# Turning f32 rows on the tensor engine: a product with a scaled identity, or a scaling on ACT and a transposition

## The chip, the cores and the metric

The kernel runs on one core of one Trainium2 chip. The metric is the device time of one execution in microseconds (us); the kernel before takes 4029.41 us (median of 3 runs, 4027.86 to 4030.45). The engines named below are PE (TensorE, products into PSUM; PEld are its weight loads), DVE (VectorE), ACT (ScalarE), POOL (GpSimd) and SP (SyncE, which here only issues DMAs). Each works through its own instructions in order; semaphores order them across engines.

## The reference, cut to what matters

```python
# x: (8, 16, 512, 512) f32
# layer 0
x = x + irfftn(complex_conv3x3(rfftn(_gn(x)), w_real, w_imag, b_real, b_imag))
# layer 1
x = x + mean_filter(_gn(x), 15)      # 15x15 box, zero padded, per channel
# _gn(v): per image and group of 2 channels, (v - mean) / sqrt(var + 1e-5)
```

Only layer 1 is concerned: the image is normalised, averaged over 15x15 pixels, and added to itself.

## The kernel before, in words

The eight images are done one after the other. An image stays in SBUF as `img`, 128 partitions (8 bands of rows x 16 channels) by T = 64 row steps by 512 columns: row step u holds row u of every band. So a sum over rows of the image is a sum over u, with a hand-over to the neighbouring band at the borders, and a sum over columns runs along the free axis.

Layer 0 rewrites `img` in place. Layer 1 then forms the box in two parts, row step by row step:

- The sum over 15 rows is never held. PSUM accumulates the whole box in `p0[0]`, and each step u adds only the difference between the row that enters and the row that leaves.
- For u from 8 to 56 (49 steps, `R < u < T - R` with R = 7) both rows are in the same band: POOL's `difference` (L1353) writes `diff[u % 2]` = row u+7 less row u-8. For the 7 steps at either border the two rows lie in different bands, and PE combines them by two products with permutation matrices ("dual-term" steps); step 0 is a sum made earlier (`head`, `tail`).
- PE turns the difference, 4 blocks of 128x128 f32: `turn_row` (L655) takes the row's block as the stationary operand and a matrix as the moving one, into `turned_ps[u % 2]`. The matrix is an identity times the scale of the normalisation (`turn_mat["ident"]`, made once per image from column 10 of `sc`), so that turn and scaling are one. The two factors of an f32 product appear in the trace as two records per product.
- ACT copies the turned row to f16 (`high_part`, L844, recorded under L727), DVE writes the rest (`low_part`, L1213), together `parts[u % 2]`.
- PE's `box_row` (L677) multiplies both parts with a 0/1 band matrix, 8 products, and accumulates in `p0[0]`; DVE's `add_box` (L1226) adds the result to the image row, and SP stores it, two rows at a time.

PE's order is: turn u+1, box u, and, while another image follows, one half of the weighted row sums of the next image (`sum_part`, L491) from u = 17 on. Box u waits for the low part of u and for addition u-1, which reads the only accumulator. Turn u+1 waits for the low part of u-1. DVE's order is: low part u, addition u-1, and from u = 16 on the statistics of one row of the next image (`count_row`, L973). ACT issues the next image's loads, 4 rows in two DMAs after every fourth high part (`load_next`, L860). POOL's difference u waits for turn u-2, since it reuses the buffer.

All code is written out in this order; no scheduler moves anything. The last image has no successor: no sums, statistics or loads.

Of the kernel before, what the change touches and what calls it, by code (L numbers as in the profile page):

```python
# [36 lines left out]
P = 128  # L37
# [4 lines left out]
T = H // HB  # L42
# [5 lines left out]
R = K // 2  # L48
# [4 lines left out]
NDIFF = T - K  # L53
LAG = 16
NQ = W // P
# [97 lines left out]
def build(nc, x, w_real, w_imag, b_real, b_imag, tab, bd_dram, out):  # L153
    x_v = x.rearrange("b c (s hl t) w -> b s c hl (t w)", s=2, hl=HL)
    out_v = out.rearrange("b c (s hl t) w -> b s c hl (t w)", s=2, hl=HL)
    with ExitStack() as ctx:
        def sb(name, shape, dt=F32):
            return ctx.enter_context(nc.sbuf_tensor(name, shape, dt))

        def sem(name):  # L160
            return ctx.enter_context(nc.semaphore(name))
# [3 lines left out]
        tb = {n: sb(n, list(tab[n].shape), tab[n].dtype) for n in TABLES if n not in IN_DRAM}  # L165
# [13 lines left out]
        diff = [piece[s] for s in range(2)]  # L179
# [15 lines left out]
        turn_mat = {n: flat_bd[:, i * P:(i + 1) * P]  # L195
                    for i, n in enumerate(("ident", "neg_ident", "neg_prev", "next_"))}
# [18 lines left out]
        sc = sb("sc", [P, 28])  # L215
# [10 lines left out]
        turned_ps = [h_ps[:, s, :].rearrange("p (k m) -> p k m", k=NQ) for s in range(2)]  # L226
# [35 lines left out]
        moved, presummed, head_ready, tail_ready = sem("moved"), sem("presummed"), sem("head_ready"), sem("tail_ready")  # L262
# [1 line left out]
        mats_ready, mean_made, mean_spread = sem("mats_ready"), sem("mean_made"), sem("mean_spread")  # L264
        mean_kept, bordered = sem("mean_kept"), sem("bordered")
        turned, high_done, low_done, banded = sem("turned"), sem("high_done"), sem("low_done"), sem("banded")
        row_kept = sem("row_kept")
        row_out, stores_held, half_seen = sem("row_out"), sem("stores_held"), sem("half_seen")
        stored = [sem(f"stored{s}") for s in range(NS)]

# [134 lines left out]
        def _(pe):  # L405
# [75 lines left out]
            def sum_part(b, q, part):  # L481

                k, r = q * 2 // CHUNK, q * 2 % CHUNK
                if part == 0:
                    wait_rows(pe, b, 2 * q)
                    if r == 0:
                        pe.wait_ge(uvw_ready, b * NCH + k + 1)
                cols = slice(part * HALF, (part + 1) * HALF)
                for i in range(2):
                    w = uvw[k % 2][:, 4 * (r + i):4 * (r + i) + 4, :].rearrange("p j c -> p (j c)")  # L490
                    m = mm(uv_ps[i * HP:(i + 1) * HP, cols], w, img[:, 2 * q + i, cols],  # L491
                           start=(q == 0 and part == 0), stop=(q == T // 2 - 1 and part == 1),
                           skip_group_check=True)
                if r == CHUNK - 2 and part == 1:
                    m.then_inc(uv_summed, 1)

            def sum_rows(b, k):

                for q in range(k * CHUNK // 2, (k + 1) * CHUNK // 2):
                    for part in range(2):  # L500
                        sum_part(b, q, part)
# [151 lines left out]
            def layer1(b, follow):  # L653

                def turn_row(u, *terms):  # L655
                    for k in range(NQ):
                        for i, (mat, row) in enumerate(terms):
                            m = mm(turned_ps[u % 2][:, k, :], row[:, k * P:(k + 1) * P], mat,  # L658
                                   start=(i == 0), stop=(i == len(terms) - 1))
                    m.then_inc(turned, 1)  # L660

                def turn_step(u):

                    if u >= 2:
                        pe.wait_ge(low_done, b * T + u - 1)
                    if u <= R:
                        turn_row(u, (turn_mat["ident"], img[:, u + R, :]),
                                 (turn_mat["neg_prev"], img[:, u + T - R - 1, :]))
                    elif u < T - R:
                        pe.wait_ge(moved, b * NDIFF + u - R)  # L670
                        turn_row(u, (turn_mat["ident"], diff[u % 2]))
                    else:
                        pe.wait_ge(row_kept, b * R + u - (T - R) + 1)
                        turn_row(u, (turn_mat["next_"], kept_row[u - (T - R)]),
                                 (turn_mat["neg_ident"], img[:, u - R - 1, :]))

                def box_row(u):  # L677

                    pe.wait_ge(low_done, b * T + u + 1)
                    pe.wait_ge(row_out, PRIMED + b * T + u)  # L680
                    for k in range(NQ):
                        lo, hi = max(k * P - R, 0), min(k * P + P + R, W)
                        for l in range(2):
                            m = mm(p0[0][:, lo:hi], parts[u % 2][:, l, k, :],  # L684
                                   tb["band16"][:, lo - k * P + R:hi - k * P + R],
                                   start=(u == 0 and k == 0 and l == 0),
                                   stop=(u == T - 1 and k == NQ - 1 and l == 1), skip_group_check=True)
                    m.then_inc(banded, 1)


                pe.wait_ge(head_ready, b + 1)
                pe.wait_ge(tail_ready, b + 1)
                turn_row(0, (tb["ident"][:], head[:]), (tb["prev"][:], tail[:]))
                pe.wait_ge(mean_made, b + 1)
                mm(c_ps[:, 24:24 + C], sc[:, 24:25].broadcast_to([P, P]), mean_in[:], start=True, stop=True).then_inc(mean_spread, 1)
                pe.wait_ge(mats_ready, b * 4 + 2)
                for u in range(T):
                    if u + 1 < T:
                        if u + 1 == T - R:
                            pe.wait_ge(mats_ready, b * 4 + 4)  # L700
                        turn_step(u + 1)
                    box_row(u)
                    if follow and u > LAG:
                        sum_part(b + 1, (u - LAG - 1) // 2, (u - LAG - 1) % 2)
                if follow:
                    sum_part(b + 1, (T - LAG) // 2 - 1, 1)
                    for k in range((T - LAG) // CHUNK, NCH):
                        sum_rows(b + 1, k)
                    input_statistics(b + 1)
# [7 lines left out]
            with pe.Fori(0, B - 1) as b:  # L717
                layer0(b)
                layer1(b, True)
            layer0(B - 1)  # L720
            layer1(B - 1, False)


        @block.scalar
        def _(act):
            def copy(out_, in_):
                return nc.scalar.activation(out_, in_, ACT.Identity)  # L727
# [15 lines left out]
            def image(b, follow):  # L743
# [95 lines left out]
                def scaled(out_, in_, scale, bias=None):  # L839
                    if bias is None:  # L840
                        return nc.scalar.activation(out_, in_, ACT.Identity, scale=scale)
                    return nc.scalar.activation(out_, in_, ACT.Identity, bias=bias, scale=scale)

                def high_part(u):  # L844
                    if R < u < T - R or u == 0:
                        act.wait_ge(turned, b * T + u + 1)
                    else:
                        act.wait_ge(bordered, b * (2 * R) + (u if u <= R else u - (T - R) + R + 1))
                    if u >= 2:
                        act.wait_ge(banded, b * T + u - 1)  # L850
                    copy(parts[u % 2][:, 0], turned_ps[u % 2]).then_inc(high_done, 1)
# [8 lines left out]
                def load_next(t, rows, signal):  # L860

                    act.wait_ge(row_out, PRIMED + b * T + t + rows)
                    if t + rows <= NDIFF:
                        act.wait_ge(moved, b * NDIFF + t + rows)
                    for i in range(2):
                        act.dma_start(img[i * HP:(i + 1) * HP, t:t + rows, :].rearrange("p t w -> p (t w)"),
                                      x_v[b + 1, i, :, :, t * W:(t + rows) * W]).then_inc(signal, 16)

                for u in range(1, T):
                    high_part(u)  # L870
                    if u <= R:
                        copy(kept_row[u - 1], img[:, u - 1, :]).then_inc(row_kept, 1)
                    if follow:
                        k = u // CHUNK - 2
                        if u % CHUNK == CHUNK - 1 and 0 <= k < NCH - LAG // CHUNK:
                            load_next(k * CHUNK, CHUNK, loaded[k])
                        if u >= T - R and u % 2 == 1:
                            load_next(u - R - 2, 2, loaded_pair[(u - (T - R)) // 2])
                            if u >= T - R + 2:
                                load_next(u - 3, 2, loaded_pair[(u - (T - R)) // 2 + 3])  # L880
# [519 lines left out]
```

## Time and profile before

| | |
|---|---|
| median of 3 runs | 4029.41 us |
| the profiled execution's own time | 4030.95 us |
| its span (first to last instruction) | 4028.9 us |
| PE, DVE busy | 87%, 86% of the span |
| POOL, ACT busy | 65%, 59% |
| loads of 512 KB in the page's list of DMA issues (ACT's queue, L866) | 7.3 us from issue to landing, median |
| layer 1 of image 0: first turn to last low part | 512.71 to about 662 us |

The page's shares are of the whole span; layer 0 and layer 1 use the engines differently, so the stretches of layer 1 are read apart. A PE "matmul" row gives the time of an instruction including its latency, and matmuls overlap, so the time PE needs for a group is read from the starts of successive groups or from the chain. The granted clock is a share of 2.4 GHz. ACTq and SPq rows are DMA issues on the queue of ACT and SP.

### The profile page before, as it was taken

Reading aid. Unit: us, or ns where it says so; the run is one execution under the profiler, and the core shown is the slowest. Engines: PE = TensorE matmul, PEld = TensorE weight load, DVE = VectorE, ACT = ScalarE, POOL = GpSimd, SP = SyncE. Lnnn points to the kernel's source line nnn. Section 1 sums busy time; section 2 is a strip of 40 time slices with the busy share of each in tenths; the row PEclk is TensorE's granted clock in tenths of the full one; section 3 lists DMA queues with packets and bytes.
Section 4 is the critical chain, followed back from the end, with each engine's and each line's share of the span. In section 5 each row is a group of like instructions: output and inputs, shape, how many; then the busy total and the mean of one; then the engine's idle time right before and its main releaser. Section 6 shows DMA issues by size and latency. Waiting matters only on the chain.

```text
span 4028.9 us, 122552 instructions
## 1 busy us (share of the span) xinstructions
PE 3515.2 (87%) x42592; PEld 2538.7 (63%) x42592; DVE 3445.0 (86%) x6382; ACT 2382.8 (59%) x3774; POOL 2638.3 (65%) x2177
## 2 busy tenths in 40 slices
PE   3199889998999989899798998999898998999988
PEld 1166576665766667666675666666576665766667
DVE  7889977998779978899788997789977998789976
ACT  0078733886248852588427883288733886248852
POOL 5088853887538865588546885388853986538865
PEclk8599999999999999999999999999999999999999
DMA  6511166111741128311382114711165111741114
GB/s 161 169 43 53 44 173 178 52 53 34 225 135 52 52 57 245 91 51 52 100 239 57 51 53 141 208 45 53 42 184 167 52 52 38 222 134 51 52 53 137
DMA packets 228530, 407.91 MB, mean 101 GB/s; under 512 B 98160, under 2 KB 173520, under 8 KB 215888
## 3 DMA queue, kind: packets, MB, share of 16 engines
q1 hardware_dynamic: 205776, 285.88, 24.6%
q10 hardware_dynamic: 22400, 117.46, 10.9%
q8 instruction: 204, 3.34, 0.4%
q14 instruction: 150, 1.23, 0.1%
HBM read 256.31 MB, written 146.80 MB: 100 GB/s over the span
## 4 chain that ended last, share of the span: by engine, by line
PE 52%; DVE 21%; issue 11%; POOL 8%; ACT 5%; ACTq 1%; DVEq 1%; SPq 1%; DMA 0%; POOLq 0%
PE h_ps L658 14%; PE p L549 11%; PE h_ps L453 9%; PE p L684 6%; PE p L491 4%; POOL ob_all L1306 3%; DVE arena L1104 3%; DVE ob_all L1152 3%; DVE half_row L1171 3%; PE xt_ps L443 3%; DVE img L1161 2%; POOL ob_all L1308 2%; POOL arena L1299 2%; DVE ob_all L1231 2%; ACT arena L727 1%
## 5 line engine op out<-in xcount | busy, mean ns | idle before, releaser
L549 PE MATMUL p<-arena,bd_all 64*64 64x512 f16 x16896 | 1206.4, 379 | 30.0 <-DVE ob_all L1152 29.6
L1299 POOL TENSOR_TENSOR arena<-arena 128x512 f16<-128x512 f32 x512 | 594.1, 1160 | 495.7 <-ACT arena L760 476.2
L453 PE MATMUL h_ps<-hilbert,arena 128*128 128x256 f16 x6144 | 754.5, 272 | 115.8 <-DVE arena L1104 111.9
L549 PEld LDWEIGHTS p<-arena,bd_all 64*64 64x64 f16 x16896 | 604.4, 106 | 385.6 <-issue 38.8
L453 PEld LDWEIGHTS h_ps<-hilbert,arena 128*128 128x128 f16 x6144 | 564.0, 97 | 398.7 <-issue 317.9
L1357 POOL TENSOR_TENSOR arena<-img 128x512 f32<-128x512 f32 x392 | 499.0, 1274 | 469.4 <-PE h_ps L658 443.9
L727 ACT ACTIVATE arena<-h_ps 128x512 f16<-128x512 f32 x512 | 305.7, 597 | 841.4 <-PE h_ps L658 593.9
L1308 POOL TENSOR_TENSOR ob_all<-ob_all,img 128x512 f32<-128x512 f32 x512 | 662.7, 1294 | 75.6 <-POOL ob_all L1306 60.6
L1306 POOL TENSOR_TENSOR ob_all<-ob_all 128x512 f32<-128x512 f32 x512 | 655.8, 1281 | 52.5 <-DVE ob_all L1152 51.9
L766 ACT ACTIVATE arena<-xt_ps 128x1024 f16<-128x1024 f16 x512 | 520.7, 1017 | 35.5 <-PE xt_ps L443 35.5
L658 PE MATMUL h_ps<-bd_all,arena 128*128 128x128 f32 x3584 | 539.5, 286 | 0.0
L783 ACT ACTIVATE img<-img,half_row (+1 forms) x1024 | 487.3, 533 | 74.5 <-DVE half_row L1171 74.5
L1215 DVE TENSOR_TENSOR arena<-h_ps,arena 128x512 f16<-128x512 f32 x512 | 353.3, 690 | 207.0 <-ACT arena L727 205.5
L658 PEld LDWEIGHTS h_ps<-bd_all,arena 128*128 128x128 f32 x3584 | 447.6, 191 | 121.2 <-issue 115.4
L774 ACT ACTIVATE arena<-h_ps 128x512 f16<-128x512 f32 x512 | 305.0, 596 | 319.7 <-PE h_ps L453 319.5
L1146 DVE SCALAR_TENSOR_TENSOR ob_all<-p,bias_c,cosw 128x256 f32<-128x256 f32 x1024 | 445.6, 477 | 33.8 <-PE p L549 29.6
L757 ACT ACTIVATE arena<-img,sc 128x512 f16 (+1 forms) x512 | 436.0, 852 | 37.0 <-POOL arena L1299 37.0
L1152 DVE SCALAR_TENSOR_TENSOR ob_all<-p,bias_c,cosw 128x256 f32<-128x256 f32 x1024 | 443.5, 475 | 0.0
L760 ACT ACTIVATE arena<-img,sc 128x512 f32 (+1 forms) x512 | 437.7, 855 | 4.2 <-POOL arena L1299 4.2
L1164 DVE BATCH_NORM_STATS2 stat<-img (+1 forms) x512 | 355.5, 694 | 52.1
L684 PE MATMUL p<-band,arena 128*128 128x135 f16 (+1 forms) x4096 | 332.5, 225 | 59.9 <-DVE ob_all L1231 58.3
L491 PE MATMUL p<-img,bd_all 128*64 128x256 f32 x2048 | 308.2, 408 | 75.1 <-POOL bd_all L1278 48.5
(163 smaller groups left out, 4980.6 us busy)
## 6 DMA issues: line engine op xcount, KB each, us to landing
out<-ob_all SPq DMA_DIRECT2D x512, 256.0 KB, 4.2
bd_all<-bd_dram SPq DMA_DIRECT2D x512, 192.0 KB, 2.3
img<-in_x ACTq DMA_DIRECT2D x168, 512.0 KB, 7.3
img<-in_x ACTq DMA_DIRECT2D x112, 256.0 KB, 4.8
wrap_mat<-tab_wrap_h SPq DMA_DIRECT2D x512, 32.0 KB, 2.0
img<-in_x SPq DMA_DIRECT2D x24, 512.0 KB, 23.1
bd_dram<-ob_all SPq DMA_DIRECT2D x16, 768.0 KB, 3.5
img<-in_x SPq DMA_DIRECT2D x16, 256.0 KB, 7.2
```

Of the source, the lines that this page charges most:

```text
L453: m = mm(dst(a), xT[:, 4 * lx + k, 0:rows], tb["hilbert16"][:, lt, k, 0:cols], start=(half == 0 and i == 0), stop=(half == 1 and i == 2))
L491: m = mm(uv_ps[i * HP:(i + 1) * HP, cols], w, img[:, 2 * q + i, cols], start=(q == 0 and part == 0), stop=(q == T // 2 - 1 and part == 1), ...
L549: m = mm(bank[out_half * HP:(out_half + 1) * HP, :], bd[s % RB][rows, 6 * lm + (j if own else j + 1), :], part, start=opens and i3 == 0, s ...
L658: m = mm(turned_ps[u % 2][:, k, :], row[:, k * P:(k + 1) * P], mat, start=(i == 0), stop=(i == len(terms) - 1))
L684: m = mm(p0[0][:, lo:hi], parts[u % 2][:, l, k, :], tb["band16"][:, lo - k * P + R:hi - k * P + R], start=(u == 0 and k == 0 and l == 0), ...
L766: nc.scalar.activation(xT.rearrange("p k (s m) -> p k s m", s=2)[:, :, ::-1, :], xt_ps[:].rearrange("p k (s m) -> p k s m", s=2), ACT.Iden ...
L783: ins = nc.scalar.activation(row, row, ACT.Identity, bias=half_row[:, s, a:a + 1])
L1152: ins = V.scalar_tensor_tensor(t2[:, a, :], p2[:, a * HALF:(a + 1) * HALF], bias_c[:, 0, t, 1 - a:2 - a], sinw[:, a, :], ALU.add, ALU.mult)
L1299: G.tensor_tensor(gp[s][:, 1, :], g32, gp[s][:, 0, :], ALU.subtract).then_inc(g_split, 1)
L1306: G.tensor_tensor(q, term_row[s % 2][0], term_row[s % 2][1], ALU.add).then_inc(t_added, 1)
L1308: G.tensor_tensor(q, q, parity(img[:, t, :]), ALU.add).then_inc(q_done, 1)
L1357: G.tensor_tensor(diff[u % 2], img[:, u + R, :], img[:, u - R - 1, :], ALU.subtract).then_inc(moved, 1)
```

## The change

For the 49 single-term steps ACT multiplies `diff[u % 2]` in place by the scale, and PE turns it with its transposition of f32 blocks against the plain identity `tb["ident"]`. PE waits for a new semaphore, `row_scaled`, in place of `moved`. Everything else stays, also the matrix `turn_mat["ident"]`, which the border steps use.

```diff
+                def turn_plain(u):
+                    for k in range(NQ):
+                        m = nc.tensor.transpose(turned_ps[u % 2][:, k, :], diff[u % 2][:, k * P:(k + 1) * P],
+                                                tb["ident"][:])
+                    m.then_inc(turned, 1)
...
                     elif u < T - R:
-                        pe.wait_ge(moved, b * NDIFF + u - R)
-                        turn_row(u, (turn_mat["ident"], diff[u % 2]))
+                        pe.wait_ge(row_scaled, b * NDIFF + u - R)
+                        turn_plain(u)
...
+                def scale_row(u):
+
+                    act.wait_ge(moved, b * NDIFF + u - R)
+                    scaled(diff[u % 2], diff[u % 2], sc[:, 10:11]).then_inc(row_scaled, 1)
+
                 for u in range(1, T):
+                    if R < u + 1 < T - R:
+                        scale_row(u + 1)
                     high_part(u)
```

PE, single-term steps while another image follows, before. `h_ps` is the PSUM tensor of the turned row, `bd_all` holds the scaled identity, `arena` the difference and the parts, `p_0` the box, `p_1` the sums:

```order
L670 REGISTER_ALU [waits low_done]
L658 MATMUL h_ps<-bd_all,arena 128x128 [waits moved]
L658 MATMUL h_ps<-bd_all,arena 128x128 x3
L679 REGISTER_ALU
L684 MATMUL p_0<-band,arena 128x135 [waits row_out,low_done]
L684 MATMUL p_0<-band,arena 128x135
L684 MATMUL p_0<-band,arena 128x142 x4
L684 MATMUL p_0<-band,arena 128x135 x2
L491 MATMUL p_1<-img,bd_all 64x256 x2
```

The same place after:

```order
L676 REGISTER_ALU [waits low_done]
L664 MATMUL h_ps<-ident,arena 128x128 [waits row_scaled]
L664 MATMUL h_ps<-ident,arena 128x128 x3
L685 REGISTER_ALU
L690 MATMUL p_0<-band,arena 128x135 [waits row_out,low_done]
L690 MATMUL p_0<-band,arena 128x135
L690 MATMUL p_0<-band,arena 128x142 x4
L690 MATMUL p_0<-band,arena 128x135 x2
L491 MATMUL p_1<-img,bd_all 64x256 x2
```

The four turning products become four transpositions in the same place and wait for ACT's scaling in place of POOL's difference; box and sums stay where they were.

ACT at the issue of the next image's loads, before (L727 is the high part, L866 the load):

```order
L846 REGISTER_ALU
L727 ACTIVATE arena<-h_ps 128x512 [waits banded,turned]
L864 REGISTER_ALU [waits row_out]
L866 ISA [waits moved]
L866 DMA img<-in_x 64x1x2048
L866 ISA
L866 DMA img<-in_x 64x1x2048
L846 REGISTER_ALU
L727 ACTIVATE arena<-h_ps 128x512 [waits banded,turned]
```

The same place after (L847 is the scaling, L733 the high part, L872 the load):

```order
L877 REGISTER_ALU
L847 ACTIVATE arena<-arena,sc 128x512 [waits moved]
L852 REGISTER_ALU
L733 ACTIVATE arena<-h_ps 128x512 [waits banded,turned]
L872 ISA [waits moved,row_out]
L872 DMA img<-in_x 64x1x2048
L872 ISA
L872 DMA img<-in_x 64x1x2048
L877 REGISTER_ALU
L847 ACTIVATE arena<-arena,sc 128x512 [waits moved]
L852 REGISTER_ALU
L733 ACTIVATE arena<-h_ps 128x512 [waits banded,turned]
```

Each high part now has the scaling of the following row queued ahead of it, and behind a load's two DMAs the first thing in the queue is a scaling.

## Rows read from the trace of the kernel before

**Rows 1.** Windows: length, PE, PEld, DVE, ACT, POOL busy, clock, DMA, GB/s:

```profile
505.00:514.00 9.00, 2.47 (x10) 2.33 (x11) 6.73 (x19) 2.29 (x6) 5.34 (x5) 0.50 0.00 0
...
534.00:548.00 14.00, 11.21 (x117) 10.21 (x115) 9.11 (x14) 5.30 (x9) 8.74 (x8) 1.00 0.64 177
548.00:560.00 12.00, 10.79 (x107) 8.93 (x106) 10.03 (x16) 2.99 (x5) 8.14 (x8) 1.00 1.02 287
560.00:640.00 80.00, 79.48 (x720) 59.72 (x720) 67.85 (x108) 21.50 (x36) 49.26 (x44) 1.00 0.82 236
...
3915.00:4000.00 85.00, 71.89 (x736) 65.81 (x736) 59.31 (x93) 27.18 (x47) 58.05 (x47) 1.00 0.46 143
```

**Rows 2.** Chain that ended last, image 0: start us, us, what:

```profile
567.15 0.58 PE p L491 x4
567.73 1.09 PE h_ps L658 x8
568.82 0.49 PE p L684 x8
```

**Rows 3.** Timeline, image 0: start us, us, engine, line, operation, [idle before]:

```profile
566.60 0.60 ACT L727 ACTIVATE arena<-h_ps 128x512 f16<-128x512 f32 x1 [1.56 <-PE h_ps L658]
...
566.80 1.57 ACTq L866 DMA_DIRECT2D img<-in_x  x2
...
567.23 0.69 DVE L1215 TENSOR_TENSOR arena<-h_ps,arena 128x512 f16<-128x512 f32 x1 [0.27 <-ACT arena L727]
567.83 0.68 DVE L1231 SCALAR_TENSOR_TENSOR ob_all<-p,img 128x512 f32<-128x512 f32 x1
```

**Rows 4.** Timeline, last image, layer 1:

```profile
3960.21 1.11 PE L658 MATMUL h_ps<-bd_all,arena 128*128 128x128 f32 x8
...
3961.40 1.27 POOL L1357 TENSOR_TENSOR arena<-img 128x512 f32<-128x512 f32 x1 [0.89 <-PE h_ps L658]
...
3963.38 0.50 PEld L684 LDWEIGHTS p<-band,arena 128*128 128x128 f16 x8 [0.72 <-DVE arena L1215]
...
3963.84 0.97 PEld L658 LDWEIGHTS h_ps<-bd_all,arena 128*128 128x128 f32 x8
...
3966.28 0.68 DVE L1231 SCALAR_TENSOR_TENSOR ob_all<-p,img 128x512 f32<-128x512 f32 x1
...
3967.07 0.50 PEld L684 LDWEIGHTS p<-band,arena 128*128 128x128 f16 x8 [0.72 <-DVE arena L1215]
```

**Rows 5.** Timeline: f16 transpositions of layer 0; two-term turns in layer 1:

```profile
304.27 0.54 PEld L443 LDWEIGHTS xt_ps<-ident,arena 128*128 128x128 f16 x8
...
512.71 0.77 PE L658 MATMUL h_ps<-ident,arena 128*128 128x128 f32 x2 [3.66 <-DVE arena L1236]
...
516.25 0.45 PE L695 MATMUL p<-mean_in,sc 128*128 128x16 f32 x2
...
531.66 1.86 PEld L658 LDWEIGHTS h_ps<-bd_all,img 128*128 128x128 f32 x16
```

**Rows 6.** ACT by line and form: busy us, mean ns, idle before:

```profile
L842 ACT ACTIVATE arena<-arena,sc 128x512 f32<-128x512 f32 x8 | 6.5, 813 | 11.9 <-DVE sc L1027 11.9
...
L812 ACT ACTIVATE wrap_high<-p,sc 128x512 f16<-128x512 f32 x8 | 5.5, 688 | 0.0
```

**Rows 7.** Timeline, ACT, two activations back to back:

```profile
529.17 0.60 ACT L727 ACTIVATE arena<-h_ps 128x512 f16<-128x512 f32 x1 [1.41 <-DVE h_ps L1223]
...
529.67 0.62 ACT L727 ACTIVATE arena<-img 128x512 f32<-128x512 f32 x1
```

**Rows 8.** Timeline, ACT's queue and the activation behind, image 0:

```profile
557.51 2.33 ACTq L866 DMA_DIRECT2D img<-in_x  x2
...
560.01 0.60 ACT L727 ACTIVATE arena<-h_ps 128x512 f16<-128x512 f32 x1 [2.12 <-PE p L684]
...
637.72 2.50 ACTq L866 DMA_DIRECT2D img<-in_x  x2
```

**Rows 9.** Windows, columns as in rows 1, between layer 1 and layer 0:

```profile
676.00:680.00 4.00, 1.60 (x9) 1.04 (x7) 2.10 (x13) 1.72 (x4) 0.00 (x0) 1.00 0.86 242
```

More of the change, by code:

```diff
@@ L266, in build @@
         turned, high_done, low_done, banded = sem("turned"), sem("high_done"), sem("low_done"), sem("banded")
-        row_kept = sem("row_kept")
+        row_kept, row_scaled = sem("row_kept"), sem("row_scaled")
         row_out, stores_held, half_seen = sem("row_out"), sem("stores_held"), sem("half_seen")
```

## The prediction

> **What bounds the kernel now.** I read the page's busy shares first: PE 87% of the span, DVE 86%. Two engines so close say only that the answer is in the stage, so I went to the windows. Layer 1 of an image that has a successor gives, for 560 to 640, PE busy 79.48 of 80 us at granted clock 1.00, with 108 DVE instructions [rows 1]: three per row, so 36 rows, 2.22 us each. In the same stage of the last image (3915 to 4000) PE is busy for 71.89 of 85, so something else paces it. Hence two regimes, read separately.
>
> For the images with a successor, the chain that ended last is PE alone: 0.58 for the weighted sums of the next image (L491), 1.09 for the single-term turn (L658), 0.49 for the box (L684) [rows 2]; over many rows the box must take 2.22 - 0.58 - 1.09 = 0.55. PE is the limit. ACT's high part takes 0.60, DVE's low part starts 0.03 later and the addition 0.60 after that [rows 3]. After every fourth high part ACT's queue issues two loads: begun 0.20 after the high part's start, 1.57 long [rows 3].
>
> Without a successor the box starts at 3963.38 and again at 3967.07 after two rows, 3.69, that is 1.845 per row, each time after a wait for DVE [rows 4]. Here the loop is turn, high part, low part, addition, box.
>
> An image has 49 single-term rows, 8 to 56. I count some 39 with the L491 sums (the 2.22 regime), 10 before them, with loads but without sums.
>
> **The change, part by part.** *PE's turn.* Removed: 8 records of L658 per row, 1.09. Added: 4 transpositions. The trace has no f32 transposition. Bounds: eight f16 transpositions' weight loads take 0.54 [rows 5], so four at that pitch take 0.27; at the other end the f32 operand costs what the product does, 1.09. A dual-term row issues 16 records in 1.86 [rows 5], 0.116 each; four at that pitch are 0.46. An f16 operation is one record, an f32 product two; whether an f32 transposition is one is my assumption (rival 1 is its failure). I take 0.45, four records at the pitch of the nearest row (f32, same size).
> The Trainium skill, "TensorE: Matmul & The Clock Gate", section Terms, calls the transpose mode 4 times faster for FP32. By it the turn would be 1.09/4 = 0.27, and the time below 23 us lower; that coincides with my low end.
>
> *ACT's scaling.* Added: one 128x512 f32 activation per single-term row, SBUF to SBUF, scale from a column. Such a copy without a column takes 0.62, a read from PSUM without one 0.60 [rows 7], and one with a column 0.688 [rows 6]; so a column costs 0.09: 0.71. Bounds 0.62 and 0.81, the latter the head's scaling with two columns [rows 6]. It blocks ACT for 0.61, since the next activation starts 0.10 before the former's end (529.17 + 0.60 against 529.67 [rows 7]). ACT has room in total: 4 x (0.61 + 0.50) + 1.57 = 6.0 per four rows, where PE before takes 8.9. But the place in the queue counts.
>
> *The added wait.* The scaling of row u+1 is queued ahead of the high part of row u, and it waits for POOL's difference of u+1, which waits for turn u-1. Behind it on ACT stand the high part, then the loads; DVE waits for that high part, PE for DVE. PE's turn u+1 now waits for the scaling, with box u queued behind it. Followed step by step, from the end of turn u:
> - difference u+2: 0.08 + 1.27, ends at 1.35;
> - scaling u+2: 0.05 + 0.61, at 2.01 ACT is free;
> - high part u+1: 0.60, at 2.61;
> - low part u+1: 0.03 + 0.61, at 3.25 DVE may start the next;
> - addition u: 0.68, at 3.93; 0.12 to PE's box u+1;
> - box u+1: 4.05 to 4.60; sums: 0.58, 5.18; turn u+3: 0.45 + 0.10 of latency, 5.73.
> The steps between are read off the last image (turn to 3960.21 + 1.11 = 3961.32, POOL from 3961.40; addition 3966.28 + 0.68, box 3967.07 [rows 4]) and off image 0 (high part 566.60, low part 567.23, addition 567.83 [rows 3]). The 0.05 from POOL to ACT I take as the like of these. Turn u+3 comes three rows after turn u: 5.73/3 = 1.91 per row with sums. Without them, with the box at 0.46 (3963.38 to 3963.84 [rows 4]), 5.06/3 = 1.69. DVE's own floor is 3 x 0.61 = 1.83, POOL's 1.27 plus a little: both lower.
>
> *The loads on ACT.* With 1.91 per row, high part u starts 0.10 after the end of turn u (2.01 less one row). The hold runs for 0.20 + 1.75 from there. Why 1.75: most holds are like that of rows 3, 1.57, and of the ten in this stretch of image 0 the longest are 2.33 and 2.50 [rows 8]; so the mean lies somewhat above the common value. The next activation started 0.17 after the hold of 2.33 [rows 8]: so at 2.22, though scaling u+2 was ready at 1.40. Late by 0.82 once in four rows: 0.20 per row. Before, this hold lay wholly under PE's box, sums and turn. So the loaded regime goes at 2.11, not 1.91.
>
> *DMA.* 2.11 instead of 2.22 raises 236 GB/s to 248; 548 to 560 shows 287 at share 1.02 [rows 1], which I take for the ceiling, at 1.82 us per row. Loads land in 7.3 us in the median (the page's list of DMA issues) and are used five rows after issue, 10.5 us: enough.
>
> **The sum.** Rows with sums: (2.22 - 2.11) x 39 = 4.3 us per image, x 7 = 30. Rows 8 to 17 with loads but without sums: before 117 PE records, 16 per row, in 14 us [rows 1], 1.91; after 1.69 and by the same working about 0.22 for the hold, 1.91: nothing. Last image, 48 rows x (1.845 - 1.69) = 7. Dual-term rows, 2 x 7 per image, keep their 16 records, nothing. Layer 0 is not touched and begins when layer 1 ends, so all of it reaches the end: 37 us, 0.9%. The profiled execution took 4030.95 (span 4028.9), 1.5 over the median of 4029.41: 3994 for it, 3992 on the median's scale.
>
> Ends of each unknown, with (39 + 10) x 7 + 48 = 391 rows on the three-row loop: turn 0.27: -0.06 x 391 = -23; turn 1.09: +0.21 x 391 = +82; scaling 0.62 or 0.81: -12 or +13; hold 1.57: -0.045 x 273 = -12; hold 2.50 throughout: +0.19 x 273 = +52. The range below is made of these.
>
> **Rivals.**
> 1. *The transposition costs what the product did.* For: it is the same size and type, and LDWEIGHTS of f32 is part of it. Against: nothing in the trace, only that a transposition has no products to sum. The loop is then 6.37/3 = 2.12, plus 0.20 for the hold: 2.32 against 2.22. Time: 3992 + 82 = 4074, slower than before. Deciding point: a turn of 0.78, where the loaded rows reach 2.22.
> 2. *The loads hold ACT longer.* This is the one mechanism on the slow side that needs no odd price: the loads come closer together, the rings are fuller, holds near 2.50 (seen once in image 0 [rows 8]) become the rule. Price 3992 + 52 = 4044. It decides from a hold of about 2.2: there the loaded rows are at 2.22. Against: most holds are 1.57 while DMA is at 0.82.
> 3. *ACT's queue is no obstacle*: holds overlap more than I reckon, and DVE's 1.83 is the limit. (2.22 - 1.83) x 39 x 7 = 106, with the last image's 7: 3916. For: DVE's operations follow each other 0.60 apart [rows 3]. Against: the loop above.
> 4. *PE falls to its lower clock.* With fewer records PE has gaps in every row. The first turn, at a granted clock of 0.50 [rows 1], the 1.2 GHz level, issues its 16 records in 3.54 us (512.71 to 516.25), 0.22 each against 0.116 at 1.00, the 2.4 GHz level [rows 5], about twice the price: 2 x (0.54 + 0.58 + 0.45) = 3.1 per row, +0.9 x 273: 4240. Against: 676 to 680 has PE busy 1.60 of 4 us at clock 1.00 [rows 9], and no gap in the new rows is above 1 us. The same page of the Trainium skill, section Part 4: PE-mode transpose, says that transposes do not count as activity for the clock gate; by it the last image, with only box products left, would be the first to fall. f16 transpositions run at 1.00 here, but between products.
> 5. *Hidden*: gains and losses cancel within 8 us, the hold near 2.1.
>
> **Chances.** Forecast 0.60 (3950 to 4015); rival 3 0.12; rival 2 0.13; rival 1 0.05; rival 4 0.03; rival 5 0.07. A measurement of this kernel can tell 0.2%, 8 us, from nothing. Faster: 0.60 + 0.12 and 0.04 of rival 2's milder holds, 0.76; within 8 us 0.08; slower 0.16. The range, 3940 to 4040, leaves out rival 1, rival 4, the far part of rival 3 and half of rival 2.
>
> **What would show it.** In the profile after: the turn's group at x4 with an issue near 0.45; ACT scaling near 0.71; in a loaded image's stretch of single-term rows about 2.1 us per row, PE busy clearly below 99%, and after every fourth high part the scaling begun late, with DVE's low part waiting for ACT; in the last image 1.69 per row; clock 1.00; holds near 1.57. Wrong if the turn is 0.8 or more, if holds grow past 2.2, if the loaded rows stay at 2.2, or if the last image gains nothing.

## The result, and the profile after

| | before | after |
|---|---|---|
| median (4 runs each) | 4028.64 us | 3978.90 us |
| lowest to highest | 4022.97 to 4030.45 | 3978.67 to 3979.86 |
| ratio, 95% interval | | 0.9879 [0.9862, 0.9896] |
| span of the profiled execution | 4028.9 us | 3978.0 us |

The changed kernel is 1.2% faster. The forecast was 3992 with a range of 3940 to 4040: the sign was right and the time lies in the range; the gain was 50 us where 37 were worked out. The cheaper turn and the hold of ACT by the loads are there as forecast. The loop that was to set the rows is another one than the forecast's.

Windows of layer 1 of image 0, after, with the columns of [rows 1]:

```profile
505.00:514.00 9.00, 2.62 (x11) 2.48 (x12) 6.58 (x19) 2.13 (x6) 5.20 (x4) 0.50 0.00 0
...
534.00:548.00 14.00, 8.27 (x93) 6.60 (x91) 10.34 (x16) 10.19 (x18) 9.97 (x9) 1.00 0.66 188
548.00:560.00 12.00, 8.65 (x85) 5.93 (x85) 10.09 (x17) 7.87 (x13) 8.38 (x8) 1.00 0.96 302
560.00:634.00 74.00, 64.01 (x567) 39.35 (x568) 65.97 (x106) 42.13 (x69) 47.74 (x43) 1.00 0.87 249
```

PE was busy for 79.48 of 80 us in [rows 1]; now it is for 64.01 of 74, and no engine is full. DVE has 106 instructions, three per row: 35.3 rows in 74 us, 2.09 each, forecast 2.11. The granted clock is 1.00 (the level of 2.4 GHz) in these windows of image 0 and in the whole of the last image's single-term rows. Rival 4 rested on a lasting fall to the lower level, and that does not come. Short falls do: five of 3.4 us each in the single-term rows of images 1, 2, 3 and 6, at 1029.8, 1057.1, 1507.7, 1968.5 and 3408.9, where the kernel before has none. Windows of image 1, columns as above:

```profile
1051.00:1057.00 6.00, 3.79 (x34) 2.31 (x36) 3.94 (x7) 2.94 (x5) 3.00 (x3) 1.00 0.90 246
1057.20:1060.30 3.10, 3.10 (x20) 2.00 (x16) 2.20 (x5) 0.82 (x2) 1.89 (x2) 0.50 0.63 211
```

Shortly before each fall PE had a pause of 1.2 to 1.9 us (here 1.25 us, up to 1056.22, behind a hold of ACT's queue of 3.11); behind other pauses, of up to 1.45, no fall came. As an estimate, half of 5 x 3.4, some 8 us, is the most that the falls can have cost; no run separates it. The Trainium skill ("TensorE: Matmul & The Clock Gate", section Part 4: PE-mode transpose) says that transposes do not count as activity; here f32 ones alternate with box products in the last image without a fall, and so they do in all single-term rows of the kernel loads_sp_sums below. No run tells whether the transpositions have a part in the five falls.

The same stretch by line, after (line, engine, operation, tiles, count, busy us, mean ns, idle time before and its releaser):

```profile
L847 ACT ACTIVATE arena<-arena,sc 128x512 f32<-128x512 f32 x34 | 24.5, 722 | 26.9 <-POOL arena L1370 24.8 <-issue 2.1
L1228 DVE TENSOR_TENSOR arena<-h_ps,arena 128x512 f16<-128x512 f32 x35 | 24.1, 689 | 8.0 <-ACT arena L733 6.3
L690 PE MATMUL p<-band,arena 128*128 128x135 f16 (+1 forms) x287 | 23.3, 224 | 9.8 <-DVE ob_all L1244 8.3
L664 PE MATMUL h_ps<-ident,arena 128*128 128x128 f32 x140 | 23.0, 287 | 1.0 <-ACT arena L847 1.0
L664 PEld LDWEIGHTS h_ps<-ident,arena 128*128 128x128 f32 x140 | 14.7, 141 | 14.6 <-issue 11.2 <-ACT arena L847 3.4
```

The scaling takes 0.722 (forecast 0.71). 140 records for 35 rows are four per row, where [rows 2] have eight: an f32 transposition is one record. The box now waits for DVE's addition (L1244), the low part for ACT's high part (L733), and the scaling for POOL's difference. Those are the edges of the loop of the prediction, but the first two belong to another loop as well (three_buffers below), so these rows do not say which of the two sets the pace.

The timeline after, one group of four rows around a load (start us, us, engine, line, operation, count, idle before and its releaser):

```profile
569.78 0.65 PE L690 MATMUL p<-band,arena 128*128 128x135 f16 x8
...
571.09 0.72 ACT L847 ACTIVATE arena<-arena,sc 128x512 f32<-128x512 f32 x1 [0.75 <-POOL arena L1370]
...
571.72 0.58 ACT L733 ACTIVATE arena<-h_ps 128x512 f16<-128x512 f32 x1
...
571.81 0.65 PE L690 MATMUL p<-band,arena 128*128 128x135 f16 x8 [0.21 <-DVE ob_all L1244]
571.83 1.85 ACTq L872 DMA_DIRECT2D img<-in_x  x2
...
573.76 0.65 PE L690 MATMUL p<-band,arena 128*128 128x135 f16 x8
573.79 0.72 ACT L847 ACTIVATE arena<-arena,sc 128x512 f32<-128x512 f32 x1 [1.49 <-POOL arena L1370]
...
574.41 0.58 ACT L733 ACTIVATE arena<-h_ps 128x512 f16<-128x512 f32 x1
...
575.02 0.72 ACT L847 ACTIVATE arena<-arena,sc 128x512 f32<-128x512 f32 x1
575.03 0.69 DVE L1228 TENSOR_TENSOR arena<-h_ps,arena 128x512 f16<-128x512 f32 x1 [0.81 <-ACT arena L733]
...
576.46 0.65 PE L690 MATMUL p<-band,arena 128*128 128x135 f16 x8 [0.88 <-DVE ob_all L1244]
...
578.25 0.65 PE L690 MATMUL p<-band,arena 128*128 128x135 f16 x8
```

Read the start of the box (L690): 569.78, 571.81, 573.76, 576.46, 578.25. The step of 2.70 is the row behind the load. The load holds ACT's queue from 571.83 to 573.68, the scaling starts at 573.79, 0.11 after it, though the row names POOL as its releaser (a wait of several is put down to one, and POOL's difference had ended long before). High part, low part and box are then late one after the other. The next step is only 1.79: the two rows take 4.49 where two undisturbed ones take 3.9, and so 0.6 is lost, not 0.74.

Steps per row, from the starts of the low parts in the profiled executions (the mean over the seven images with a successor, and the last image):

| row steps | before | after | forecast |
|---|---|---|---|
| 18 to 55, with loads and sums | 2.241 | 2.087 | 2.11 |
| 9 to 17, with loads | 1.97 | 1.85 | 1.91 |
| 8 to 17, all ten together | 18.9 | 18.3 | unchanged |
| last image, 18 to 55 | 1.855 | 1.722 | 1.69 |
| 56 to 63, all but one dual-term, together | 23.9 | 23.9 | unchanged |
| from an image's last low part to the next one's first (layer 0) | 337.5 | 337.7 | unchanged |

From first to last low part a loaded image goes from 145.3 to 138.7 (-6.6, x 7 = -46) and the last from 125.4 to 119.4 (-6.0). That is the 51 us between the spans, within 1. The step of rows 9 to 17 flatters the change: in the means of the seven images the step to row 8, just ahead, grew from 1.21 to 1.62, and that to row 9 fell from 2.49 to 1.57.

In the last image the steps after are 1.62, 1.59 and 1.94, over and over: a loop that closes every three rows. Before they were 1.53 and 2.16 in turn, a loop that closes every two.

### The profile page after: what moved, and what is told of

The parts are those of the page before. It is cut to its first block, busy times and chain, and to the rows that moved or that the text cites. A ratio compares the mean times of both kernels' runs of the same rounds, so it can differ in the third digit from the quotient of the medians.

```text
span 3978.0 us, 120151 instructions
## 1 busy us (share of the span) xinstructions
PE 3352.9 (84%) x41024; PEld 2324.7 (58%) x41024; DVE 3436.7 (86%) x6382; ACT 2628.2 (66%) x4166; POOL 2636.2 (66%) x2177
## 3 DMA queue, kind: packets, MB, share of 16 engines
q8 instruction: 195, 3.19, 0.3%
## 4 chain that ended last, share of the span: by engine, by line
PE 42%; DVE 21%; POOL 15%; issue 14%; ACT 5%; DMA 2%; DVEq 1%; ACTq 1%; SPq 1%; POOLq 0%
PE p L549 13%; PE h_ps L453 11%; POOL arena L1370 8%; PE h_ps L658 6%; DVE arena L1117 3%; PE xt_ps L443 3%; DVE half_row L1184 3%; DVE ob_all L1165 3%; PE p L690 2%; POOL ob_all L1319 2%; DVE img L1174 2%; POOL arena L1312 2%; POOL ob_all L1321 2%; DVE ob_all L1244 1%; PE h_ps L549 1%
## 5 line engine op out<-in xcount | busy, mean ns | idle before, releaser
L733 ACT ACTIVATE arena<-h_ps 128x512 f16<-128x512 f32 x512 | 300.5, 587 | 285.9 <-DVE h_ps L1236 201.9
L690 PE MATMUL p<-band,arena 128*128 128x135 f16 (+1 forms) x4096 | 336.0, 226 | 165.5 <-DVE ob_all L1244 152.9
L847 ACT ACTIVATE arena<-arena,sc 128x512 f32<-128x512 f32 x392 | 282.8, 721 | 257.3 <-POOL arena L1370 239.2
L690 PEld LDWEIGHTS p<-band,arena 128*128 128x128 f16 x4096 | 261.4, 98 | 254.7 <-DVE arena L1228 150.8
```

Of the source, the lines that this page charges most:

```text
L690: m = mm(p0[0][:, lo:hi], parts[u % 2][:, l, k, :], tb["band16"][:, lo - k * P + R:hi - k * P + R], start=(u == 0 and k == 0 and l == 0), ...
```

## The experiments

Each kernel was timed in three rounds against the kernel before on the same chip. All ratios are to that. "Loaded" is the step of rows 18 to 55, "last" that of the last image, in the profiled execution. The median of the kernel before moved by some 4 us from one set of runs to the next (4026.5, 4023.8, 4027.5), so differences are read from ratios.

| kernel | us | ratio, 95% | loaded | 9 to 17 | last |
|---|---|---|---|---|---|
| product | 4047.87 | 1.0055 [1.0038, 1.0072] | 2.298 | 1.95 | 1.885 |
| scale_after | 3995.79 | 0.9930 [0.9913, 0.9947] | 2.024 | 2.05 | 2.016 |
| three_buffers | 3970.34 | 0.9865 [0.9848, 0.9881] | 2.095 | 1.81 | 1.595 |
| loads_sp | 3946.16 | 0.9802 [0.9785, 0.9818] | 1.975 | 1.75 | 1.722 |
| three_sp | 3941.24 | 0.9784 [0.9768, 0.9801] | 1.984 | 1.70 | 1.595 |
| scale_end | 3955.98 | 0.9828 [0.9812, 0.9845] | 2.024 | 1.81 | 1.635 |
| loads_sp_sums | 3897.30 | 0.9684 [0.9668, 0.9700] | 1.797 | 1.75 | 1.723 |
| scale_end_sp_sums | 3907.05 | 0.9705 [0.9689, 0.9721] | 1.850 | 1.75 | 1.636 |
| before_loads_sp | 4019.63 | 0.9981 [0.9972, 0.9991] | 2.222 | 1.92 | 1.856 |
| three_sp_sums | 3890.66 | 0.9664 [0.9648, 0.9681] | 1.814 | 1.67 | 1.595 |

**product**: half of the change. ACT scales, PE turns by the f32 product with the plain identity.

```diff
-                        turn_plain(u)
+                        turn_row(u, (tb["ident"][:], diff[u % 2]))
```

> ACT's scaling stays; the 49 single-term turns are f32 products with the plain identity again, in place of transpositions. Theory (a loop over three rows: difference, scaling, high part, low part, addition, box, sums, turn; plus a hold of ACT by the loads): the turn takes 1.09 again in place of 0.66, so +0.14 us per row over 391 rows, +56: 4035 us; rows of the last image from 1.72 to 1.86 us, loaded rows from 2.09 to about 2.23. Rival 'DVE or DMA paces the loaded rows now': loaded rows stay at 2.09, only the last image loses, 3986. Rival 'the scaling alone is what pays': 3979.

Measured 4047.87: scaling and wait alone cost 0.55%, 22 us, and the transposition then gives back 1.0055 - 0.9879 = 1.76%, 71 us. The window 560 to 620 has PE still nearly full, with small gaps:

```profile
560.00:620.00 60.00, 57.48 (x518) 42.75 (x516) 48.86 (x79) 33.45 (x53) 37.28 (x33) 1.00 0.81 232
```

The direction was right, the size too small (4035 expected): against the kernel before, scaling and wait cost 2.298 - 2.241 = 0.06 per loaded row. Why the loaded rows went to 2.298 and not to 2.23 was not followed up.

**scale_after**: ACT does the scaling of u+1 behind the high part of u, no longer ahead of it.

```diff
-                    if R < u + 1 < T - R:
-                        scale_row(u + 1)
                     high_part(u)
+                    if R < u + 1 < T - R:
+                        scale_row(u + 1)
```

> The same instructions as the changed kernel, but ACT scales row u+1 behind the high part of row u, not ahead of it. Theory: the difference then is no longer in the way of the high part, but a loop of one row appears: high part 0.50, scaling 0.72, turn 0.66 and 0.06 of hand-over, 1.94 per row. Last image from 1.72 to 1.94 (+10 us); loaded rows stay near 2.1, since a hold still delays the next high part; rows 8 to 17 lose 0.1 each (+7): about 3997 us. Rival 'the place in the queue does not matter, ACT has room': 3979.

The total is as expected (3995.79). The rows that make it up are not quite: without sums the steps rise to 2.02 (expected 1.94), the loaded ones fall to 2.024. Order on ACT matters in both directions: ahead, it delays the high part behind a load, behind, it delays the next turn. That reading of the loaded rows was not tested by itself.

**three_buffers**: a third difference buffer, so that POOL's difference u waits for turn u-3, no longer for turn u-2.

```diff
-                diff = [piece[s] for s in range(2)]
+                diff = [piece[0], piece[1], piece[10]]
...
-                    if u >= R + 3:
-                        pool.wait_ge(turned, b * T + u - 1)
+                    if u >= R + 4:
+                        pool.wait_ge(turned, b * T + u - 2)
```

> POOL's difference has three buffers in place of two, so it waits for turn u-3 and not u-2. Nothing else changes. Theory: this opens the three-row loop, the scaling is ready long before ACT reaches it. Last image: next loop is box, turn, high part, low part, addition and box over two rows, 0.46 + 0.66 + 0.03 + 0.60 + 0.03 + 0.61 + 0.68 + 0.12 = 3.19, 1.60 per row, -6 us. Loaded rows: DVE's 1.83 plus what a hold costs when DVE has no room to catch up (1.95 + 0.17 + 0.61 after the high part against 1.83, 0.9 in four rows), 2.05, -9; rows 8 to 17 -7: about 3957 us. Rival 'the hold alone makes the difference to DVE's floor': 3979, last image unchanged at 1.72. Rival 'DMA paces': last image only, 3973.

3970.34, 13 above the expected 3957, and by the ratio not to be told from the changed kernel (0.9865 and 0.9879, the intervals overlap). The steps say more. In the last image the step falls from 1.722 to 1.595 as expected, and the pattern of three rows is gone: there the loop over POOL was the limit. In the loaded rows nothing falls (2.087 and 2.095), which speaks against the account on which the forecast of 1.91 rested; three_sp below shows the same without the holds. What replaces it is another loop, seen in this kernel's last image (timeline, columns as above):

```profile
3880.36 0.65 PE L690 MATMUL p<-band,arena 128*128 128x135 f16 x8 [0.50 <-DVE ob_all L1244]
...
3880.84 0.60 PE L664 MATMUL h_ps<-ident,arena 128*128 128x128 f32 x4
...
3881.49 0.60 ACT L733 ACTIVATE arena<-h_ps 128x512 f16<-128x512 f32 x1 [0.38 <-PE h_ps L664]
...
3882.11 0.69 DVE L1228 TENSOR_TENSOR arena<-h_ps,arena 128x512 f16<-128x512 f32 x1 [0.30 <-ACT arena L733]
...
3882.72 0.68 DVE L1244 SCALAR_TENSOR_TENSOR ob_all<-p,img 128x512 f32<-128x512 f32 x1
...
3883.55 0.65 PE L690 MATMUL p<-band,arena 128*128 128x135 f16 x8 [0.50 <-DVE ob_all L1244]
```

Box u, turn u+2, high part u+2, low part u+2, then on DVE, queued behind that low part, addition u+1, for which box u+2 waits: 3883.55 - 3880.36 = 3.19 for two rows, 1.595 per row, which is the measured step.

**loads_sp**: SP issues the loads of the next image, behind its stores, and ACT none.

```diff
-                            load_next(k * CHUNK, CHUNK, loaded[k])
...
                     store(b, j, j % NS)
+                    k = (j - 4) // 2
+                    if j % 2 == 0 and 0 <= k < NCH - LAG // CHUNK:
+                        sp.wait_ge(moved, b * NDIFF + (k + 1) * CHUNK)
+                        for i in range(2):
+                            sp.dma_start(...).then_inc(loaded[k], 16)
```

> The next image's loads of rows 0 to 47 are issued by SP, behind the store of the same row, in place of ACT. The scaling stays. Theory: the hold is gone, loaded rows go at the three-row loop with a turn of 0.66, 5.84/3 = 1.95 in place of 2.09, -36 us, rows 8 to 17 at 1.72 in place of 1.85, -8; last image unchanged: about 3935 us. Rival 'DMA paces the loaded rows': unchanged 3979 or slower, since the same bytes move. Rival 'the loop, not the hold, gives 2.09': 3979.

3946.16, another 0.8%. The loaded step goes to 1.965 in five of the seven images and 2.00 in two. So the hold of ACT's queue cost 2.087 - 1.975 = 0.11 per row, 0.45 per load. Every row is now like the next (timeline of image 1, columns as above):

```profile
1073.29 0.65 PE L696 MATMUL p<-band,arena 128*128 128x135 f16 x8
...
1073.87 0.65 PE L497 MATMUL p<-img,bd_all 128*64 128x256 f32 x4
...
1074.45 0.66 PE L670 MATMUL h_ps<-ident,arena 128*128 128x128 f32 x4
...
1075.17 0.58 ACT L739 ACTIVATE arena<-h_ps 128x512 f16<-128x512 f32 x1
...
1075.78 0.69 DVE L1232 TENSOR_TENSOR arena<-h_ps,arena 128x512 f16<-128x512 f32 x1
...
1076.38 0.68 DVE L1248 SCALAR_TENSOR_TENSOR ob_all<-p,img 128x512 f32<-128x512 f32 x1
...
1077.21 0.65 PE L696 MATMUL p<-band,arena 128*128 128x135 f16 x8
```

It is the same two-row loop with the sums in it (L497, 0.58): 0.58 + 0.58 + 0.72 + 0.61 + 0.60 + 0.83 = 3.92, 1.96 per row.

**three_sp**: both edits, to see whether the two loops bind one behind the other.

> Three difference buffers and the loads issued by SP. With SP's loads alone the loaded rows measured 1.965 us, which fits the three-row loop (5.84/3 = 1.95) and also a two-row loop that needs neither difference nor scaling: box 0.58, sums 0.58, turn 0.66, hand-over 0.06, high part 0.60, 0.03, low part 0.60, addition 0.68, 0.14: 3.93/2 = 1.965. Theory 'both bind': opening the three-row loop leaves loaded rows at 1.96; last image 1.60 (-6), rows 8 to 17 from 1.74 to 1.62 (-8): about 3932 us against loads_sp's 3946. Rival 'the three-row loop alone': loaded rows fall to DVE's 1.83, -34 more, 3898.

The loaded step stays at 1.965 to 2.00 and only rows without sums gain. 3941.24 in all, where 3932 was expected; by the ratio alone it can't be told from loads_sp. With the POOL loop gone nothing changes in the loaded rows: the two-row loop is enough to set them. In loads_sp the loop over POOL stood within 0.02 of it (5.84/3 = 1.95).

**scale_end**: no scaling on ACT at all. PE turns the raw difference, and DVE's addition multiplies by a column in place of a constant (the border matrices lose their scale).

```diff
-                                           p0[0], 1.0 / (K * K * BOX_SCALE), img[:, u, :],
+                                           p0[0], sc[:, 25:26], img[:, u, :],
...
-                    if R < u + 1 < T - R:
-                        scale_row(u + 1)
```

> No scaling on ACT at all: differences, border matrices and means are left unscaled, and DVE's addition multiplies the box by the scale's column in place of a constant (the same sums, in another place). Transposition stays, loads stay on ACT. Theory (loops and hold): without scaling the three-row loop is gone and the high part u+1 is due 1.96 after the high part u, the hold ends 1.95 + 0.17 after it: late 0.16 in four rows, loaded rows 2.0 in place of 2.09 (-23), rows 8 to 17 near 1.7 (-10), last image 1.60 (-6), if the addition with a column is not longer: about 3938 us. Rival 'the hold alone keeps the loaded rows at 2.09, whatever stands behind it': 3963. A column in the addition could cost 0.06, as one row in two loops: +10.

3955.98, better than after by 0.5%, though 18 us short of the expectation. Its sum left out the column's price on DVE, which it named as a possible 10 us; the rest is rows that fell less than expected (loaded 2.024 for 2.0, rows 9 to 17 1.81 for 1.7). The addition over the whole run, this kernel and then after:

```profile
L1243 DVE SCALAR_TENSOR_TENSOR ob_all<-p,sc,img 128x512 f32<-128x512 f32 x512 | 380.2, 743 | 12.9 <-PE p L690 6.5 <-DMA out<-ob_all 5.9 <-issue 0.3
```

```profile
L1244 DVE SCALAR_TENSOR_TENSOR ob_all<-p,img 128x512 f32<-128x512 f32 x512 | 348.7, 681 | 8.5 <-PE p L690 4.5 <-DMA out<-ob_all 3.7
```

The column costs 62 ns per addition. The addition lies in the two-row loop: (3.19 + 0.06)/2 = 1.625 against 1.635 measured in the last image.

**loads_sp_sums**: loads on SP, and the sums moved from behind box u to ahead of it, behind turn u+1.

```diff
-                    box_row(u)
                     if follow and u > LAG:
                         sum_part(b + 1, (u - LAG - 1) // 2, (u - LAG - 1) % 2)
+                    box_row(u)
```

> As loads_sp, and PE does the sums of the next image between turn u+1 and box u, not behind box u. Theory: the sums leave both loops (two-row loop 3.93 - 0.58 = 3.35, 1.68 per row; three-row loop 5.84 - 0.58 = 5.26, 1.75), DVE's three operations then bind, 1.83: -0.13 x 39 x 7 = -36 from 3946, about 3910 us. Rival 'DMA': 60 us of loaded rows in loads_sp moved 270 GB/s at share 0.95; the ceiling of 287 to 302 GB/s gives 1.74 to 1.83 per row, so stores or loads may hold rows at 1.85 to 1.9: 3920 to 3930. Rival 'PE is full as it was': PE busy 56.29 of 60 there, 3946.

3897.30, ratio 0.9684. The sums now lie where PE waited for DVE, the loop loses their 0.58, and DVE becomes the limit: 59.58 of 60 us busy.

```profile
560.00:620.00 60.00, 55.39 (x533) 35.65 (x532) 59.58 (x101) 39.84 (x67) 45.06 (x40) 1.00 1.00 290
```

Three operations follow each other 0.60 apart, 1.797 per row. This is rival 3's number (1.83), reached only with the two obstacles removed. It also gives the cleanest price of the turn, since the sums follow it directly:

```profile
1060.47 0.60 PE L670 MATMUL h_ps<-ident,arena 128*128 128x128 f32 x4
...
1061.01 0.65 PE L497 MATMUL p<-img,bd_all 128*64 128x256 f32 x4
```

1061.01 - 1060.47 = 0.54 for four transpositions. The four records start 0.11 apart ((0.60 less the 0.27 of one) / 3); the other 0.2 lies between the last of them and the sums.

**scale_end_sp_sums**: the three edits at once.

> No scaling on ACT (the addition scales), loads on SP, sums between turn and box. Theory: loaded rows at DVE's 1.83 as in loads_sp_sums, rows 8 to 17 from 1.74 to 1.62, last image from 1.72 to 1.60: 3910 - 8 - 6 = 3896 us. Rival 'DMA': loaded rows at 1.9, about 3915. If the addition is longer by 0.06 for its column, DVE's floor is 1.89 and the time 3912.

3907.05, slower than the kernel with the last two alone. Where DVE is the limit, its 62 ns count in full: 1.797 + 0.06 = 1.86 against 1.850. Scaling on ACT, which has room, is then the better place.

**before_loads_sp**: the kernel before, with only the loads moved to SP.

> The kernel before (product with the scaled identity, no scaling on ACT) with the one edit that gained 2% on the changed kernel: the next image's loads are issued by SP, ACT issues none. Theory: with the products PE is the limit of the loaded rows (0.58 + 1.09 + 0.55 = 2.22 to 2.24), and the hold of ACT's queue lies under it, so taking it away gains nothing: loaded rows stay at 2.24, time within 0.2% of before. Rival: the hold costs 0.14 per row there too; then loaded rows fall to 2.10 and the time by 38 x 7 x 0.14 = 37 us, ratio 0.991, and the 0.8% that the loads on SP gave the changed kernel would be owed to it alone, whatever turns the rows.

4019.63, ratio 0.9981: 0.2%, where the same edit is worth 0.8% on the changed kernel. The loaded step is 2.222 in every image, and PE is busy 60.00 of 60 us:

```profile
1050.00:1110.00 60.00, 60.00 (x546) 45.24 (x545) 51.28 (x82) 16.12 (x27) 38.32 (x34) 1.00 0.87 239
```

The full window does not show that PE is the limit, since busy time counts each product's latency. The starts tell more (timeline, columns as above):

```profile
1070.46 0.65 PE L690 MATMUL p<-band,arena 128*128 128x135 f16 x8
...
1071.62 1.16 PE L664 MATMUL h_ps<-bd_all,arena 128*128 128x128 f32 x8
...
1072.82 0.60 ACT L733 ACTIVATE arena<-h_ps 128x512 f16<-128x512 f32 x1 [1.66 <-PE h_ps L664]
...
1073.45 0.69 DVE L1219 TENSOR_TENSOR arena<-h_ps,arena 128x512 f16<-128x512 f32 x1 [0.37 <-ACT arena L733]
...
1074.06 0.68 DVE L1235 SCALAR_TENSOR_TENSOR ob_all<-p,img 128x512 f32<-128x512 f32 x1
...
1074.88 0.65 PE L690 MATMUL p<-band,arena 128*128 128x135 f16 x8
```

From box u to box u+2 it is 4.42, 2.21 per row, over the same two-row loop. From turn to box PE takes 1.00 in one row and 1.10 in the next, so its own work is 0.58 + 0.58 + 1.00 = 2.16 per row, 0.05 less than the loop; and all boxes of rows 20 to 54 of these seven images start 0.15 after the end of an addition on DVE, as nine of ten do in the kernel before. So this kernel's loaded rows were set by the two-row loop as well, with PE close behind it. The kernel before stood at 2.241: its cover of the hold was nearly, not wholly, complete.

**three_sp_sums**: three buffers, loads on SP, sums ahead of the box.

> All three edits on the changed kernel: three difference buffers, loads issued by SP, and the next image's sums between turn u+1 and box u. Theory: each removes a loop of its own. The loaded rows are already at DVE's floor in the kernel with the last two edits (1.80, three operations of 0.60), so the third buffer changes only the rows without sums: last image 1.72 to 1.60 x 48 rows = -6 us, rows 8 to 17 1.75 to 1.69 x 10 x 7 = -4. Ratio about 0.966, some 10 us below the kernel with two of the edits (ratio 0.9684). Rival: with POOL freed of the turn, its differences collide more with DVE's operations (both read and write the same memory), DVE's operations lengthen and the loaded rows go back above 1.85: ratio 0.97 or more.

3890.66, ratio 0.9664 [0.9648, 0.9681], the best of this study, 2.2% below the changed kernel. The last image falls to 1.595 and rows 9 to 17 to 1.67 as expected; the loaded rows are at DVE's floor with 0.02 given back. Against the kernel with two of the edits the intervals overlap, and in the profiled executions only the last image is shorter (113.9 against 119.2 us from first to last low part; a loaded image takes 126.9 against 126.6). So it is not shown that the third buffer still gains in the total.

## Why the prediction was right, and where its sizes were off

- *PE is the limit of the loaded rows before.* Nearly, but not so. The 0.55 for the box was only what was left of 2.22. By the starts PE's work is 2.16 per row, and the two-row loop through DVE's addition takes 2.21 (before_loads_sp). A PE busy for 60.00 of 60 us still waited 0.10 in every second row.
- *The turn, 0.45.* The assumption of one record per transposition held, and so did the 0.11 from record to record. The turn is still longer, 0.54 to the start of the next work, for the 0.2 behind the last record. So the turn went from 1.00 to 1.10 down to 0.54, about by half, and from first start to last end from 1.16 to 0.66. The Trainium skill ("TensorE: Matmul & The Clock Gate", section Terms) calls the transpose mode 4 times faster for FP32; by it, as an estimate, the turn would have been 0.27. The trace gives a factor of 2, and the measurement decides.
- *The scaling, 0.71 and 0.61 of ACT's queue.* Right: 0.722, and the high part starts 0.63 after it.
- *The three-row loop, 1.91.* The step that failed. It was followed over POOL alone, and the number came out near by luck: with a turn of 0.66 to its end it gives 1.95, the two-row loop over DVE's addition and PE's sums gives 1.96. The three buffers told them apart: they gained in the last image, where the loop over POOL set 1.722 (1.69 forecast, 1.72 with the turn as measured), and nothing in the loaded rows. The prediction had looked for the next limit among the waits that the change adds, not among those that were there already. The two-row loop stood in its own rows: box to box 3.69 over two rows of the last image [rows 4]. With the sums (0.58), the longer box (0.55 for 0.46) and the forecast's turn (0.55 for 1.11) that is 3.80, 1.90 per row, the same number as the forecast's 1.91 by another path. Read this way the change is simple: the turn is 0.50 shorter in a loop over two rows, 2.21 to 1.96.
- *The hold of the loads, 0.82 per four rows.* The mechanism was right, and is in the timeline as described: the load, then the scaling 0.11 after its end, then the low part waiting for ACT. The size is 0.45 per four rows (2.087 less 1.975). The holds were shorter than the 1.75 that was taken (1.60 in the mean over rows 18 to 55), which is 0.15 of the 0.37 between forecast and measurement; the rest fits the timeline, where the row behind a late one makes up part of the delay. The loaded rows came out at 2.087 against 2.11.
- *Rows 8 to 17, no gain.* Somewhat off: the ten steps went from 18.9 to 18.3 us, 0.07 per row, 5 us in seven images. The 1.91 before was read about right (1.89); after, the hold cost less than the 0.22 forecast (1.83 per row, 1.73 in loads_sp).
- *The sum.* Forecast 30 + 0 + 7. Measured by the steps: 37 x 7 x 0.154 = 40, 5 and 6, together the 51 of the spans. The 14 more are some 5 from reading 2.22 for what was 2.241 (0.021 x 259), 6 from 2.087 for 2.11, and 5 from rows 8 to 17, less 1 each for the longer turn in the last image and for two rows counted too many.
- *Rivals.* Rival 1 did not happen (four records, 0.54). Rival 2's long holds occur (3.11 once in image 1, 3.04 once in image 0) but beside ones of 1.26, not as the rule. Rival 3 is true of DVE's floor and not of this kernel. Rival 4 happened for five short stretches and not for good. Its "no gap above 1 us" was wrong, as the pause of 1.25 shows, and its sum was: +0.9 per row counts from 2.22, but was added to the time that belongs to 2.11. The chance of 0.16 for slower rested mostly on rivals 1 and 2. The point at which the change would have lost is shown by the kernel with the product: without the cheaper turn it loses 0.55%.

## What to carry to other kernels

When an engine is busy for 99% of a stretch, do not take it for the limit, and before it is relieved look for the limit among all loops through its queue, also those that are there already: walk from one instance of an instruction to the next one through every wait and every queue, and divide by the rows between. A DMA issue on a queue costs little while the loop leaves that queue idle for as long, and becomes a term as soon as the loop is shorter; here the same edit was worth 0.2% before the change and 0.8% after it. And where an engine waits in every row, put its independent work into that wait: the sums ahead of the box gave 1.2% once the loads were moved, as much as the change itself. What that edit gives with the loads still on ACT was not run.

## What the runs showed of the hardware that was not expected

- An f32 transposition of 128x128 on PE is one record, the f32 product of the same size two, and the records of both start 0.11 us apart. Four transpositions take 0.54 to the start of the next work, eight product records 1.00 to 1.10. The gain is the halved count, not a faster record.
- In the changed kernel the granted clock fell to 0.50 for 3.4 us five times, each time shortly after a pause of PE of 1.2 to 1.9 us, and was 1.00 again afterwards.
- A per-partition column as the scalar of DVE's scalar_tensor_tensor from PSUM, in place of a constant, costs 62 ns on 128x512 (681 to 743).
- The core moved 290 GB/s at a DMA share of 1.00 over 60 us in the kernel with the loads on SP and the sums moved, with DVE busy 59.58 of 60: the row took 1.80, a little less than the 1.82 that the prediction took for the ceiling of the transfers. How near that ceiling is was not measured.
